# The layer norms' normalisation goes from GpSimd to VectorE, and the chains of work around the scans are placed anew

## The chip, the core and the metric

The kernel runs on one core of one Trainium2 chip. The metric is device microseconds (us) of one launch. Five engines work side by side, each through its own instruction queue in order: TensorE (PE in the profile, PEld for its weight loads), VectorE (DVE), ScalarE (ACT), GpSimd (POOL), and SyncE (SP), which here only issues DMAs. They wait for each other through semaphores, and an instruction that waits holds up everything behind it on its engine.

## The reference

A block of three parts on 4096 tokens (2 batches of 2048) of width 256, all in float32:

```python
x = x + 0.5 * ffn(layernorm(x))      # 8 groups of 512 tokens, each with its own W1, b1, W2, b2; no activation between
x = x + ssm(layernorm(x))
x = x + 0.5 * ffn(layernorm(x))

def layernorm(x):  return (x - mean(x)) / sqrt(var(x) + 1e-5)
def ssm(x):                           # D_INNER = 512 channels, 16 states each
    x_in, z = split(x @ Wi.T + bi)
    u  = silu(conv4(x_in) + conv_b)   # causal, per channel
    dt = softplus(x_in[..., :32] @ Wdt.T + bdt)
    h  = h * exp(dt * A) + dt * Bm * u           # over time, per channel and state
    y  = sum_over_states(h * Cm)
    return (y * silu(z)) @ Wo.T + bo + x * Dv.mean()
```

## The kernel before

**Tiling.** The tokens go in four passes of 1024 (`it` 0 to 3). Each pass has four blocks of 128 channels, so there are 16 blocks `k` (k = 4 it + channel block). A block has 16 scans, s = 0 to 15, each a VectorE instruction over 128 lanes (32 channels by 4 of the 16 states) and 1024 tokens. Block 0 is halved: 32 scans of 512 tokens. That makes 272 scans, numbered i; block k from 1 on holds the scans 16k+16 to 16k+31.

**The ring around a scan.** ScalarE computes the decay `exp` of a scan into one of eight buffers G (L1003, out of RD, a copy of dt that a DMA has spread over the lanes). VectorE scans in that buffer (L1123, with RV, the spread dt*u). TensorE sums the states of four scans into Y (`red`, L1269), and then ScalarE may write the exps of four later scans into those buffers: the exps of scans i+4 to i+7 stand behind `red` of scans i-4 to i-1 in ScalarE's queue and need that sum, so a `red` that comes late on TensorE holds up ScalarE's exps and after them the scans.

**A block's other work**, done while the block before is scanned: projections on TensorE (`xim`, `zm`, `dm`, `um`), their evacuation on ScalarE (`xi`, `z`, `u`, and softplus as `dtr`, `dte`, `dtl`), two small VectorE steps between scans (`dt` L1070, `w` = dt*u L1110), the spreading DMAs (`repd`, `repw` on SyncE's queue), and at s = 3 the product with the gate (`yz` L1132), which needs the last `red` of the block before.

**Layer norms.** There are 24, numbered c = 6 it + 2 ph + hf: pass, place in the block of three (ph 0 to 2), half of 512 tokens. A norm is: on ScalarE the sum (`sum` L812, or from an evacuation) and the squares (`sq` L829, four instructions); then the small steps on [128, 4], `var` (L733), `rstd` (a power with exponent -0.5, L741), `sr` (L746), `off` (L751); then the normalisation `norm` (L758), four instructions of [128, 256] that write XN; then on TensorE the transposes `xt` (L1178), which wait for all four, and ScalarE's copies `xtc` (L849). For the norms 0 to 3, 22 and 23 (`early(c)`), which lie before the scans are in full run or behind them, the steps but `rstd` are on VectorE (`vvar` and so on, `vnorm` L1100). For the 18 norms 4 to 21 all small steps and the normalisation are on GpSimd.

GpSimd also has the second half of the merged FFN weights' mean (`msv` L788, for TensorE's transposes `mt` L1168; the merge `mm` L1158 multiplies W1 by W2 ahead of time), the skip term (`skip` L768 to L776: two small instructions, four of [128, 256] and one of [128, 1024]) and a residual addition (`res` L783).

**What sets the order.** `schedule(do)` is written once and run for each engine, which picks its own stages out of it; so each engine's queue has the stages in the order of this one list. Work besides the scans is written as chains (Python generators). After each scan, `step()` lets every open chain go on to its next `yield`. `PLAN` has the block and the s at which each chain starts, `DTS` and `PROJ` how many scans ahead of its block a block's dt chain and projection chain start, `REST`, `SHIFT` and `WAIT` how many steps a chain rests at certain places, `SENDS` after which scan the DMAs `repw` stand, `RATE` and `STORE` how much work of TensorE and ScalarE a step may let through. Where a stage stands in the list says what it stands behind; when it runs is up to its waits.

Of the kernel before, what the change touches and what calls it, by code (L numbers as in the profile page):

```python
# [6 lines left out]
ALU = mybir.AluOpType  # L7
# [37 lines left out]
        "save": (0, 10)}  # L45
RATE, STORE = 160, 190
FIRST = ["dts", "proj", "outs"]
# [7 lines left out]

PLAN = {"outs": (0, 5), "back0": (0, 12), "back1": (0, 9), "x0": (0, 0), "first0": (0, 0), "front0": (0, 1),
        "x1": (0, 8), "first1": (0, 9), "front1": (0, 11), "ln0": (1, 2), "ln1": (1, 11), "merge0": (2, 6),
        "merge1": (2, 3), "outs3": (3, 3), "skips": (3, 1)}
DTS, PROJ = -20, -25

SENDS, LATE = {6: (0, 1), 13: (2,), 14: (3,)}, {14: (0, 1, 2), 15: (3,)}
REST = 3
SHIFT = 2
WAIT = 7

# [10 lines left out]
def early(c):  # L76

    return c < 4 or c >= 22


def made(stage, c):

    return ("v" if early(c) else "") + stage

# [56 lines left out]
def schedule(do):  # L141
# [76 lines left out]
    def norm(c):  # L218
# [11 lines left out]
        yield 0  # L230
        for part in ("var", "rstd", "sr", "off", "norm"):
            do(part if part == "rstd" else made(part, c), c)
        for _ in range(0 if early(c) else WAIT - 1):
            yield 0
# [227 lines left out]
    a, b, c = norm(0), norm(1), norm(2)  # L462
# [20 lines left out]
    a = half(0, 0)  # L483
# [13 lines left out]
    for i, (k, p, s) in enumerate(UNITS):  # L497
# [8 lines left out]
        if i % 4 == 0:  # L506
            for n in range(i + LEAD, min(i + LEAD + 4, len(UNITS))):
                ko, po, _ = UNITS[n]
# [25 lines left out]
    a, b = back(3, 0), back(3, 1)  # L534
# [15 lines left out]
def build(nc, x, w, wit, wdt, wot, bo, cols, masks, out):  # L550
# [3 lines left out]
    with ctx:  # L554
# [67 lines left out]
        def tokens(c):  # L622
            it, ph, hf = c // 6, c % 6 // 2, c % 2
            return it, ph, hf, X[:, (2 * it + hf) % NX, :, :], LV[:, c % 6, :, :], XN[:, place[c] % 2, :, :]
# [94 lines left out]
        def _(eng):  # L719
            e = Engine(eng, count, sems)  # L720

            def do(stage, *a):
# [24 lines left out]
                elif stage == "off":  # L747
# [4 lines left out]
                                      ).then_inc(sems["off"])  # L752
                elif stage == "norm":
                    c, = a
                    _, _, _, v, lv, xn = tokens(c)
                    e.wait_ge("off", c)
                    for i in range(4):
                        ins = eng.tensor_scalar(xn[:, i, :], v[:, i, :], lv[:, 3, i:i + 1], lv[:, 4, i:i + 1],  # L758
                                                ALU.mult, ALU.add)
                    ins.then_inc(sems["norm"])  # L760
                elif stage == "skip":
# [247 lines left out]
        def _(eng):  # L1009
            e = Engine(eng, count, sems)  # L1010

            def do(stage, *a):
# [82 lines left out]
                elif stage == "vnorm":  # L1095
                    c, = a
                    _, _, _, v, lv, xn = tokens(c)
                    e.wait_ge("voff", c)
                    for i in range(4):
# [248 lines left out]
```

## Time and profile before

| | us |
|---|---|
| median of 3 runs (860.54 to 864.77) | 864.36 |
| the profiled execution's own time | 864.43 |
| its span in the trace, first to last instruction | 862.6 |
| VectorE busy | 666.5 (77%) |
| TensorE busy | 642.4 (74%) |
| ScalarE busy | 598.8 (69%) |
| GpSimd busy | 401.6 (47%) |

The span is split by the scans. The first scan starts at 58.7 us, block 1 at 143.1, block 15 at 785.2, and the last scan ends near 822. In 17 of the 40 slices of the page's second part VectorE is busy nine tenths and more; its idle time there lies in single stretches of 2 to 8 us. Those, and who ended them, are what the views below are asked for. In the rows, `L758` is a line of the kernel before, "xN" the number of instructions in a row that the view has put together, and "[8.30 <-X]" says that the engine was idle for 8.30 us before it and that X ended this.

### The profile page before, as it was taken

To read this page: it belongs to the slowest core of one execution; us is meant where nothing else is said; L and a number is where in the kernel's file an instruction comes from. 1 tells how busy PE (TensorE), PEld (TensorE's weight loads), DVE (VectorE), ACT (ScalarE), POOL (GpSimd) and SP (SyncE) were. 2 spreads that over 40 slices of the span, in tenths; PEclk is the share of its full clock that TensorE was granted. 3 is DMA by queue.
4 is the path that set the end of the run, shared out by engine and by line. 5 is a ranking of instruction groups with operands and counts; after the bars stand their busy time and mean duration, and the time that the engine had idled before them with its cause. 6 is when DMAs were issued, how large, how long until landed. Compare 5 with 4: busy or idle time off the path is not lost.

```text
span 862.6 us, 8004 instructions
## 1 busy us (share of the span) xinstructions
PE 642.4 (74%) x2794; PEld 320.1 (37%) x2794; DVE 666.5 (77%) x412; ACT 598.8 (69%) x1046; POOL 401.6 (47%) x232
## 2 busy tenths in 40 slices
PE   5876677959784759897686859895476797754957
PEld 4643342414241335444242336432221453310635
DVE  2424656699977985999788967989689999699920
ACT  1475577799583957979487848989397689573432
POOL 0003852432596084288997364556881049400000
PEclk9998698879886989999798979998688899785988
DMA  8242345142736150234435240415033324232001
GB/s 308 81 155 65 134 123 219 49 171 75 243 113 229 61 184 1 109 136 149 168 121 197 74 170 1 193 51 196 24 120 124 128 92 152 93 126 93 1 0 49
DMA packets 39432, 103.05 MB, mean 119 GB/s; under 512 B 4000, under 2 KB 12960, under 8 KB 38880
## 3 DMA queue, kind: packets, MB, share of 16 engines
q1 hardware_dynamic: 36832, 94.40, 29.6%
q10 hardware_dynamic: 2560, 8.14, 4.0%
q8 instruction: 22, 0.36, 0.2%
q14 instruction: 18, 0.15, 0.1%
HBM read 23.08 MB, written 4.19 MB: 32 GB/s over the span
## 4 chain that ended last, share of the span: by engine, by line
POOL 27%; ACT 23%; PE 22%; issue 18%; DVE 5%; DMA 3%; ACTq 1%; SPq 0%; POOLq 0%; DVEq 0%
POOL XN L758 12%; ACT G L1003 10%; PE Y L1269 5%; DVE G L1123 4%; POOL LV L741 3%; POOL X L772 3%; PE MB L1195 3%; PE MB L1158 2%; POOL MS L788 2%; PE MB L1236 2%; ACT XN L829 2%; POOL LV L751 2%; ACT XI L923 2%; PE MB L1178 2%; PE MB L1290 2%
## 5 line engine op out<-in xcount | busy, mean ns | idle before, releaser
L1003 ACT ACTIVATE G<-RD,COL 128x1024 f32<-128x1024 f32 (+1 forms) x272 | 276.2, 1087 | 127.8 <-PE Y L1269 124.4
L1123 DVE TENSOR_TENSOR_SCAN G<-G,STT,RV 128x1024 f32<-128x1024 f32 (+1 forms) x144 | 313.7, 2241 | 32.2 <-issue 20.4
L1123 DVE TENSOR_TENSOR_SCAN G<-G,RV 128x1024 f32<-128x1024 f32 (+1 forms) x128 | 272.9, 2192 | 19.3 <-ACT G L1003 16.3
L1269 PE MATMUL Y<-G,RW 128*32 128x512 f32 x1024 | 159.9, 730 | 67.7 <-DVE G L1123 55.1
L758 POOL TENSOR_SCALAR XN<-X,LV 128x256 f32<-128x256 f32 x72 | 137.6, 1922 | 1.9
L733 POOL TENSOR_SCALAR LV<-LV 128x4 f32<-128x4 f32 x18 | 16.7, 929 | 221.9 <-ACT XN L829 221.7
L741 POOL TENSOR_TENSOR LV<-LV,HALF 128x4 f32<-128x4 f32 x24 | 43.4, 1810 | 148.7 <-DVE LV L1078 147.1
L1269 PEld LDWEIGHTS Y<-G,RW 128*32 128x32 f32 x1024 | 31.0, 124 | 163.3 <-issue 90.7
L1236 PE MATMUL MB<-XI,DIAG 128*64 128x512 f32 x248 | 69.8, 691 | 26.9 <-DMA XI<-XI 26.9
L772 POOL TENSOR_SCALAR X<-X,LV 128x256 f32<-128x256 f32 x32 | 82.2, 2578 | 0.8
L1178 PE MATMUL MB<-COL,XN 128*128 128x128 f32 x192 | 33.6, 332 | 61.6 <-POOL XN L758 47.4
L1195 PE MATMUL MB<-MT,XF 128*128 128x256 f32 x256 | 65.9, 393 | 0.6 <-ACT XF L849 0.5
L1214 PE MATMUL MB<-XT,WI 128*128 128x512 f32 x128 | 63.4, 624 | 0.1
L1290 PE MATMUL MB<-WO,ZS 128*128 128x256 f32 x256 | 62.9, 384 | 0.0
L1247 PE MATMUL MB<-XT,WI 128*128 128x512 f32 x128 | 57.8, 599 | 0.0
L1178 PEld LDWEIGHTS MB<-COL,XN 128*128 128x128 f32 x192 | 27.6, 172 | 76.6 <-POOL XN L758 31.4
L1158 PE MATMUL MB<-W 128*128 128x257 f32 x192 | 50.9, 416 | 5.5 <-DMA W<-in_w 4.6
L1195 PEld LDWEIGHTS MB<-MT,XF 128*128 128x128 f32 x256 | 50.1, 197 | 12.3 <-issue 5.1
L829 ACT ACTIVATE XN<-X,LV 128x256 f32<-128x256 f32 x96 | 47.4, 496 | 7.6 <-POOL X L783 4.8
L1290 PEld LDWEIGHTS MB<-WO,ZS 128*128 128x128 f32 x256 | 49.8, 195 | 7.2
L1070 DVE SCALAR_TENSOR_TENSOR DW<-MB,COL,DW 128x512 f32<-128x512 f32 x32 | 22.6, 744 | 38.2 <-ACT DW L981 38.2
L788 POOL TENSOR_SCALAR MS<-MS,MV 128x256 f32<-128x256 f32 x12 | 29.3, 2447 | 39.5 <-DVE MV L1057 39.5
(86 smaller groups left out, 765.7 us busy)
## 6 DMA issues: line engine op xcount, KB each, us to landing
RD<-DW SPq DMA_DIRECT2D x60, 512.0 KB, 3.7
RV<-DW SPq DMA_DIRECT2D x60, 512.0 KB, 3.8
W<-in_w SPq DMA_DIRECT2D x48, 256.5 KB, 4.1
XI<-XI ACTq DMA_DIRECT2D x30, 256.5 KB, 3.8
X<-in_x SPq DMA_DIRECT2D x8, 512.0 KB, 4.3
out<-X SPq DMA_DIRECT2D x8, 512.0 KB, 3.0
G<-in_w SPq DMA_DIRECT2D x2, 1026.0 KB, 9.9
RV<-in_w SPq DMA_DIRECT2D x2, 1026.0 KB, 15.0
```

The lines of the kernel that those rows point to most:

```text
L741: eng.tensor_tensor(lv[:, 3, :], lv[:, 1, :], HALF[:, :], ALU.pow).then_inc(sems["rstd"])
L758: ins = eng.tensor_scalar(xn[:, i, :], v[:, i, :], lv[:, 3, i:i + 1], lv[:, 4, i:i + 1], ALU.mult, ALU.add)
L772: ins = eng.tensor_scalar(v[:, i, :], v[:, i, :], lv[:, 5, i:i + 1], lv[:, 6, i:i + 1], ALU.mult, ALU.subtract)
L829: ins = eng.activation(xn[:, i, :], v[:, i, :], ACT.Square, bias=lv[:, 0, i:i + 1], scale=-256.0, accum_out=lv[:, 1, i:i + 1])
L1003: eng.activation(G[:, i % NG, t0:t1], RD[:, q, t0:t1], ACT.Exp, scale=NAC[:, states(i):states(i) + 1]).then_inc(sems["exp"])
L1123: eng.tensor_tensor_scan(g, g, RV[:, (4 * k + q) % NR, t0:t1], STT[:, idx:idx + 1] if goes_on else 0.0, ALU.mult, ALU.add).then_inc(sems[" ...
L1158: ins = eng.matmul(bank("merge", g, i)[:, 0:257], v[:, 257 + 128 * i:385 + 128 * i], v[:, 0:257], start=(c == 0), stop=(c == 7))
L1178: ins = eng.transpose(bank("xt", c, j)[:, 128 * i:128 * i + 128], xn[:, i, 128 * j:128 * j + 128], ident)
L1195: ins = eng.matmul(o, XF[:, j, 128 * t:128 * t + 128], MT[:, g % NX, j, :], start=(i == 0 and j == 0 and not summed), stop=(i == 1 and j = ...
L1236: ins = eng.matmul(bank("um", k, hf)[64 * g:64 * g + 64, :], DIAG[:, 4 * ct + 2 * g + t, :], XI[:, g, 512 * hf + 2 * t:512 * hf + 2 * t + ...
L1269: ins = eng.matmul(Y[32 * q:32 * q + 32, 512 * h:512 * h + 512], RW[:, states(i + o), :], G[:, (i + o) % NG, 512 * h:512 * h + 512], start ...
L1290: ins = eng.matmul(o, ZS[:, (4 * it + ct) % NZ, 128 * (2 * pr + i):128 * (2 * pr + i) + 128], WO[:, ct, :], start=False, stop=(i == 1 and ...
```

## The change

Two things change. The normalisation of the 18 norms becomes a VectorE stage (`vnorm`) that stands between scans and waits for GpSimd's `off`; GpSimd keeps `var`, `rstd`, `sr` and `off` for these norms. And the numbers that place the chains are others.

```diff
-RATE, STORE = 160, 190
+RATE, STORE = 200, 100
...
-PLAN = {"outs": (0, 5), "back0": (0, 12), "back1": (0, 9), "x0": (0, 0), "first0": (0, 0), "front0": (0, 1),
...
+PLAN = {"outs": (0, 1), "back0": (0, 11), "back1": (0, 13), "x0": (0, 0), "first0": (0, 10), "front0": (0, 1),
...
-DTS, PROJ = -20, -25
+DTS, PROJ = -21, -25
-SENDS, LATE = {6: (0, 1), 13: (2,), 14: (3,)}, {14: (0, 1, 2), 15: (3,)}
-REST = 3
+SENDS, LATE = {9: (0,), 12: (1, 2), 14: (3,)}, {14: (0, 1, 2), 15: (3,)}
+REST = 4
-WAIT = 7
+WAIT = 4
...
-    return ("v" if early(c) else "") + stage
+    return ("v" if early(c) or stage == "norm" else "") + stage
...
-        for part in ("var", "rstd", "sr", "off", "norm"):
+        for part in ("var", "rstd", "sr", "off"):
             do(part if part == "rstd" else made(part, c), c)
-        for _ in range(0 if early(c) else WAIT - 1):
+        for _ in range(0 if early(c) else WAIT):
+            yield 0
+        do("vnorm", c)
+        if not early(c):
             yield 0
...
                 elif stage == "vnorm":
                     c, = a
                     _, _, _, v, lv, xn = tokens(c)
-                    e.wait_ge("voff", c)
+                    e.wait_ge(made("off", c), c)
                     for i in range(4):
                         ins = eng.tensor_scalar(xn[:, i, :], v[:, i, :], lv[:, 3, i:i + 1], lv[:, 4, i:i + 1],
                                                 ALU.mult, ALU.add)
```

In the order's rows an operation's first tile is the one written, `x4` the number in a row; a scan reads there as SCALAR_TENSOR_TENSOR on G and RV. Lines of the changed kernel are 5 lower on these engines (L1118 is the scan, L1095 the normalisation, L1264 `red`, L1173 the transposes).

**VectorE, block 4 into block 5** (`DW` is `dt` or `w`, `ZS` is `yz`). Before:

```order
L1123 SCALAR_TENSOR_TENSOR G<-G,STT,RV 128x1024
L1132 TENSOR_TENSOR ZS<-ZS,Y 128x1024
L1123 SCALAR_TENSOR_TENSOR G<-G,STT,RV 128x1024 x2
L1110 TENSOR_TENSOR DW<-DW 128x1024
L1123 SCALAR_TENSOR_TENSOR G<-G,STT,RV 128x1024 x13
L1070 SCALAR_TENSOR_TENSOR DW<-MB,COL,DW 128x512 x2
```

and changed:

```order
L1118 SCALAR_TENSOR_TENSOR G<-G,STT,RV 128x1024 x3
L1105 TENSOR_TENSOR DW<-DW 128x1024
L1118 SCALAR_TENSOR_TENSOR G<-G,STT,RV 128x1024 x2
L1095 TENSOR_SCALAR XN<-X,LV 128x256 x4
L1118 SCALAR_TENSOR_TENSOR G<-G,STT,RV 128x1024 x8
L1095 TENSOR_SCALAR XN<-X,LV 128x256 x4
L1118 SCALAR_TENSOR_TENSOR G<-G,STT,RV 128x1024
L1095 TENSOR_SCALAR XN<-X,LV 128x256 x4
```

The norms 12, 13 and 4 now stand between scans, and `w` one scan later.

**GpSimd, blocks 2 to 4** (`MS` is `msv`, the rows with DM and BO are a skip term). Before, `msv` of group 5 stands behind both skip terms of the pass:

```order
L788 TENSOR_SCALAR MS<-MS,MV 128x256 x2
L768 TENSOR_SCALAR LV<-LV,DM 128x4
L769 TENSOR_SCALAR LV<-LV,DM 128x4
L772 TENSOR_SCALAR X<-X,LV 128x256 x4
L776 TENSOR_TENSOR X<-X,BO 128x1024
L768 TENSOR_SCALAR LV<-LV,DM 128x4
L769 TENSOR_SCALAR LV<-LV,DM 128x4
L772 TENSOR_SCALAR X<-X,LV 128x256 x4
L776 TENSOR_TENSOR X<-X,BO 128x1024
L788 TENSOR_SCALAR MS<-MS,MV 128x256 x2
```

and changed, behind one:

```order
L783 TENSOR_SCALAR MS<-MS,MV 128x256 x2
L763 TENSOR_SCALAR LV<-LV,DM 128x4
L764 TENSOR_SCALAR LV<-LV,DM 128x4
L767 TENSOR_SCALAR X<-X,LV 128x256 x4
L771 TENSOR_TENSOR X<-X,BO 128x1024
L783 TENSOR_SCALAR MS<-MS,MV 128x256 x2
L763 TENSOR_SCALAR LV<-LV,DM 128x4
```

The same holds for groups 6 and 7 in blocks 6 and 7.

**TensorE, the end of block 6** (XT,WI are projections, COL,XN transposes of a norm, Y is `red`). Before, the transposes of norm 5 stand ahead of the block's last `red`:

```order
L1269 MATMUL Y<-G,RW 32x512 x8
L1204 MATMUL MB<-XT,WI 32x512 x2
L1214 MATMUL MB<-XT,WI 128x512 x2
L1178 MATMUL MB<-COL,XN 128x128 x8
L1204 MATMUL MB<-XT,WI 32x512 x2
L1269 MATMUL Y<-G,RW 32x512 x8
```

and changed, where they have gone to block 5:

```order
L1264 MATMUL Y<-G,RW 32x512 x8
L1199 MATMUL MB<-XT,WI 32x512 x2
L1209 MATMUL MB<-XT,WI 128x512 x2
L1199 MATMUL MB<-XT,WI 32x512 x2
L1264 MATMUL Y<-G,RW 32x512 x8
```

The norms 10 and 11 move like 4 and 5. At the start, the merge of group 2 (8 `mm`) moves from the first half of block 0 to its second half, and the merge of group 3 and the FFN of norm 6 from block 0 to block 1. A block's `dtl` stands one scan earlier and its `dt` where it stood. The stages behind the last scan are the same.

## Rows read from the trace of the kernel before

**Rows 1.** Busy time by stretch (start:end, length, engines, granted clock, DMA).

```profile
0.00:58.00 58.00, 41.11 (x168) 29.06 (x169) 15.93 (x43) 23.61 (x62) 3.43 (x11) 0.97 0.46 166
58.00:143.10 85.10, 63.28 (x238) 32.88 (x238) 44.69 (x49) 58.41 (x138) 42.76 (x35) 0.86 0.42 145
143.10:785.20 642.10, 484.29 (x2152) 223.21 (x2149) 563.81 (x289) 489.87 (x792) 353.35 (x184) 0.87 0.35 125
785.20:862.60 77.40, 53.67 (x240) 34.98 (x240) 42.04 (x33) 26.92 (x56) 2.03 (x2) 0.81 0.04 14
188.40:227.20 38.80, 34.89 (x160) 15.72 (x160) 38.77 (x24) 35.01 (x48) 12.73 (x9) 0.93 0.42 132
```

**Rows 2.** VectorE's waits in 143.1 to 785.2 us: total, times, longest.

```profile
DVE DW L1070 <- ACT DW L981: 23.7, 11, 5.3
DVE G L1123 <- issue: 20.4, 4, 8.3
DVE G L1123 <- ACT G L1003: 14.5, 6, 7.1
DVE ZS L1132 <- PE Y L1269: 13.2, 3, 8.0
DVE DW L1110 <- ACT DW L948: 4.9, 4, 1.3
```

**Rows 3.** Timelines by engine at 300 to 330 us (start, length, instruction, idle before).

```profile
308.30 12.49 POOL L758 TENSOR_SCALAR XN<-X,LV 128x256 f32<-128x256 f32 x4
...
320.94 1.94 PE L1178 MATMUL MB<-COL,XN 128*128 128x128 f32 x8 [9.54 <-POOL XN L758]
...
326.58 4.26 ACT L1003 ACTIVATE G<-RD,COL 128x1024 f32<-128x1024 f32 x4 [11.25 <-PE Y L1269]
...
327.81 2.35 DVE L1123 TENSOR_TENSOR_SCAN G<-G,STT,RV 128x1024 f32<-128x1024 f32 x1 [8.30 <-issue]
```

**Rows 4.** VectorE's other long waits between scans, and TensorE's for GpSimd, 143.1 to 785.2.

```profile
279.39 2.35 DVE L1123 TENSOR_TENSOR_SCAN G<-G,STT,RV 128x1024 f32<-128x1024 f32 x1 [4.69 <-issue]
...
431.40 1.22 DVE L1132 TENSOR_TENSOR ZS<-ZS,Y 128x1024 f32<-128x1024 f32 x1 [4.99 <-PE Y L1269]
...
516.93 2.29 DVE L1123 TENSOR_TENSOR_SCAN G<-G,RV 128x1024 f32<-128x1024 f32 x1 [7.10 <-ACT G L1003]
...
622.40 1.22 DVE L1132 TENSOR_TENSOR ZS<-ZS,Y 128x1024 f32<-128x1024 f32 x1 [8.01 <-PE Y L1269]
...
744.98 4.59 DVE L1123 TENSOR_TENSOR_SCAN G<-G,STT,RV 128x1024 f32<-128x1024 f32 x2 [7.13 <-issue]
...
PE MB L1178 <- POOL XN L758: 47.4, 5, 13.0
```

**Rows 5.** The normalisation on either engine: two groups of the span, two of GpSimd's timeline.

```profile
L758 POOL TENSOR_SCALAR XN<-X,LV 128x256 f32<-128x256 f32 x72 | 137.6, 1922 | 1.9
...
L1100 DVE TENSOR_SCALAR XN<-X,LV 128x256 f32<-128x256 f32 x24 | 8.3, 408 | 0.2
...
129.87 2.19 POOL L758 TENSOR_SCALAR XN<-X,LV 128x256 f32<-128x256 f32 x4
...
598.85 16.28 POOL L758 TENSOR_SCALAR XN<-X,LV 128x256 f32<-128x256 f32 x4
```

**Rows 6.** GpSimd's small steps of norms 12 and 13, and the scans beside the first.

```profile
299.80 1.66 POOL L733 TENSOR_SCALAR LV<-LV 128x4 f32<-128x4 f32 x1 [26.57 <-ACT XN L829]
...
306.04 2.15 POOL L751 TENSOR_SCALAR LV<-LV 128x4 f32<-128x4 f32 x1
...
333.86 0.79 POOL L733 TENSOR_SCALAR LV<-LV 128x4 f32<-128x4 f32 x1 [13.06 <-ACT XN L829]
...
336.11 0.20 POOL L751 TENSOR_SCALAR LV<-LV 128x4 f32<-128x4 f32 x1
...
299.14 20.36 DVE L1123 TENSOR_TENSOR_SCAN G<-G,STT,RV 128x1024 f32<-128x1024 f32 x9
```

**Rows 7.** VectorE's timeline in block 10, around GpSimd's normalisation of 598.85 us.

```profile
587.76 26.63 DVE L1123 TENSOR_TENSOR_SCAN G<-G,RV 128x1024 f32<-128x1024 f32 x12
```

More of the change, by code:

```diff
@@ L54 @@
 AT = {unit: i for i, unit in enumerate(UNITS)}
-PLAN = {"outs": (0, 5), "back0": (0, 12), "back1": (0, 9), "x0": (0, 0), "first0": (0, 0), "front0": (0, 1),
-        "x1": (0, 8), "first1": (0, 9), "front1": (0, 11), "ln0": (1, 2), "ln1": (1, 11), "merge0": (2, 6),
-        "merge1": (2, 3), "outs3": (3, 3), "skips": (3, 1)}
-DTS, PROJ = -20, -25
-SENDS, LATE = {6: (0, 1), 13: (2,), 14: (3,)}, {14: (0, 1, 2), 15: (3,)}
-REST = 3
+PLAN = {"outs": (0, 1), "back0": (0, 11), "back1": (0, 13), "x0": (0, 0), "first0": (0, 10), "front0": (0, 1),
+        "x1": (0, 2), "first1": (0, 1), "front1": (0, 10), "ln0": (1, 1), "ln1": (2, 0), "merge0": (2, 5),
+        "merge1": (1, 6), "outs3": (0, 14), "skips": (3, 10)}
+DTS, PROJ = -21, -25
+SENDS, LATE = {9: (0,), 12: (1, 2), 14: (3,)}, {14: (0, 1, 2), 15: (3,)}
+REST = 4
 SHIFT = 2
-WAIT = 7
+WAIT = 4
 def passes(k):
@@ L752, in do @@
                                       ).then_inc(sems["off"])
[L753 to L760, printed above, removed]
                 elif stage == "skip":
```

## The prediction

> **What bounds the kernel now.** I read the busy times by stretch first, then VectorE's waits, then the timelines of all engines at its longest waits.
>
> By stretch [rows 1], the columns are TensorE, its weight loads, VectorE, ScalarE, GpSimd. From block 1 to block 14 (143.1 to 785.2 us, 642.1 us) VectorE is busy 563.8 us, TensorE 484.3, ScalarE 489.9. Block 2 (188.4 to 227.2) shows the floor: VectorE is busy 38.77 of 38.80 us. So scans in a row are the bound, and what can be won between 143.1 and 785.2 us is VectorE's idle time there, 642.1 - 563.8 = 78.3 us. Ahead of 143.1 us VectorE is idle for most of the first 58 us and for 85.1 - 44.7 = 40.4 us of the next stretch; the tail of 77.4 us is the same code after the change.
>
> Who ends the 78.3 us [rows 2]: the softplus step `dt` waits for ScalarE's logarithm 11 times, 23.7 us; scans wait for "issue" 4 times, 20.4 us, and for their exp 6 times, 14.5 us; `yz` waits for TensorE's sums 13.2 us; `w` waits for silu 4.9 us. That is 76.7 of them.
>
> The views name the last link only. Followed back at one place [rows 3]: GpSimd normalises norm 12 from 308.30 to 320.79 us; TensorE has been idle for 9.54 us when it starts the transposes at 320.94; `red` stands behind them in its queue, so ScalarE's next exps start at 326.58 after 11.25 us without work, and VectorE's scan at 327.81 after 8.30 us idle. The scan does not need norm 12. It waits since TensorE's queue is blocked by a GpSimd step. There are five more such places [rows 4]: VectorE idle for 4.69 us (here TensorE waits for `msv`, which stood behind two skip terms), 4.99, 7.10, 8.01 and 7.13 us. TensorE's waits for the normalisation add to 47.4 us in five waits. The six stalls of VectorE are 8.30 + 4.69 + 4.99 + 7.10 + 8.01 + 7.13 = **40.2 us**, half of the idle time.
>
> **Why GpSimd is late.** The same four instructions take 2.19 us where VectorE is idle and 16.28 us beside scans [rows 5]; the small steps likewise. Norm 12's four run from 299.80 to 306.04 + 2.15 = 308.19, 8.4 us, those of norm 13, in one of VectorE's stalls, from 333.86 to 336.31, 2.4 us [rows 6]. The scans hardly suffer: twelve in a row over 26.63 us, 2.22 us each, with the slowest normalisation of 16.28 us beside them [rows 5, 7].
>
> **Part 1: what the normalisation costs VectorE.** 24 instructions of this kind keep VectorE busy for 8.3 us, 0.346 us each as they overlap, 0.408 us each alone [rows 5]. 18 norms have 72: between 24.9 and 29.4 us. All lie in VectorE's queue between scans, on the path. Norms 6 and 7 lie in block 0, where VectorE has 40.4 us idle [rows 1] (norm 6 stands right ahead of a `w` that waits for ScalarE); I take off 2 x 1.4 and get **+22 us** (20 to 28).
>
> **Part 2: what the new wait costs.** `vnorm` stands four scans behind `off`'s place in the list and waits for GpSimd. Everything behind it on VectorE is scans, and behind these the whole ring. Had it stood there before, norm 12 would have come up two scans into the row of nine, at 299.14 + 2 x 2.26 = 303.7 us [rows 6], and `off` ended at 308.2: 4.5 us late. But a waiting VectorE leaves GpSimd alone, and then the remaining steps run at norm 13's pace: `rstd` was under way and the two behind it take 0.20 us each with small gaps, so about 305, a wait of 1.5 us. In the new order the squares come earlier against the scans, since ScalarE is no longer held up by a blocked TensorE ahead of them, and several norms (14, 15, 17, 20, 21) have five or six scans of room. I count 0.5 us for each of 18, **+9 us**. The ends are 0, and 4.5 us each, 81 us.
>
> **Part 3: the stalls behind the normalisation.** TensorE's transposes now stand behind a step that VectorE has done in its own order, two or three scans before. `msv` of groups 5 and 7 stands behind one skip term, not two, and norms 5 and 11 no longer stand ahead of the last `red` of blocks 6 and 10. Of the 40.2 us I take back 37; the rest is for what is late next. Ends: half, 20, and all.
>
> **Part 4: `dt` and `w`.** 23.7 + 4.9 = 28.6 us in 15 waits, 1.9 us on average [rows 2]. ScalarE's logarithm stands one scan (2.2 us) earlier with `dt` where it was, and `w` one scan later. The two longest waits (to 5.3 us) follow a stall of part 3, which had put ScalarE behind. That would clear nearly all; but the norms' squares of two halves and the output's evacuations now crowd into blocks 4 and 8. I take back **18 us** (0 to 28). What remains of the 78.3 us is then 78.3 - 37 - 18 = 23 us, plus the 9 us of part 2.
>
> **Part 5: the start.** The first half of block 0 loses 8 matmul groups that stood between the transposes of norm 3 and its projections; the second half loses one merge of two and an FFN, which go to block 1. VectorE is idle 40.4 of 85.1 us there. TensorE's load in block 1 grows, but its average share of 484.3 in 642.1 us leaves room. I take **-6 us** (-12 to +4).
>
> **Part 6: scans beside GpSimd.** 137.6 us of GpSimd's work go [rows 5]; at 2.22 us a scan beside it against 38.77 us for block 2 with its 16 scans and other steps, little comes back: **-2 us** (0 to -4). The Trainium skill ("SBUF — State Buffer", where the shared port pair of VectorE and GpSimd is told) has it that the pair is an exclusive lock that a VectorE instruction with two SBUF inputs needs and a GpSimd instruction too, each blocking the other for its whole length. By that rule each of the 72 instructions, 2.19 / 4 = 0.55 us alone, would also hold a scan up, and their removal would return 40 us and not 2. The trace agrees for GpSimd's side (16.28 against 2.19 us) and not for the scans' side.
>
> The DMAs `repw` move: the first now stands behind the four `repd` on SyncE's queue, four to six scans (9 us and more) before the scan that reads it. VectorE's waits for a DMA are not among the rows of any size, so I cost this at nothing; if a transfer of the next block came late, its first scan would show it.
>
> **The sum.** 862.6 + 22 + 9 - 37 - 18 - 6 - 2 = 830.6 us of span. The profiled execution took 864.43 us with 862.6 us of span, 1.8 us more, and is within 0.1 us of the median. Forecast 832.4, rounded **832 us**, 3.7% faster.
>
> **The rivals.**
> - *The new wait takes the place of the old ones* (slower). If ScalarE's squares do not come earlier, `off` is late at most norms, and each lateness is now VectorE's own. For it: norm 12 would have been 4.5 us late as the trace stands. Against it: GpSimd speeds up while VectorE waits, and that caps it. At 3 us each (between 1.5 and 4.5) it is 54 us in place of 9: 832 + 45 = 877 us. It makes the change slower from (32 + 9) / 18 = 2.3 us a norm on.
> - *The stalls move* (no change). TensorE and ScalarE have a part of the idle time in them for their own reasons, for instance in blocks 4, 5, 8 and 9, where output projection, four norms and their FFNs now meet. Then half of 37 + 18 returns as waits for an exp or a sum: 832 + 27 = 859 us. For it: "issue" and exp waits are the least explained. Against it: three quarters load on both, and block 2 ran without a gap.
> - *All clears* (faster still). With VectorE's idle time from block 1 to 14 down to 5 us: 23 + 9 - 5 = 27 us less, 805 us. The same order of time would come of the page's rule above, with 40 us given back by the scans' side: 832 - 38 = 794 us. The trace speaks against the rule; I give the two 0.10 together.
>
> **How the numbers follow.** Forecast 0.72, stalls move 0.10, slower rival 0.08, all clears 0.10. The forecast's own cases go from 812 (all of parts 3 and 4) to 850 (part 3 at 25, part 4 at 8). To leave out no more than 2 in 10, the range runs from 806 to 858. This measurement can tell about 0.5% from no change, 860.0 to 868.7 us. Faster: 0.72 + 0.10 and a part of the second rival, 0.85; the same 0.07; slower 0.08.
>
> **What would show it.** VectorE busy near 666.5 + 25 - 2 = 690 us and its idle time between block 1 and block 14 down from 78 to about 32 us. No wait of TensorE for XN of over 2 us. The `vnorm` group at about 0.35 to 0.41 us an instruction, with an idle time ahead of it, ended by GpSimd's `off`, of some 9 us in all: over 40 us there would be the slower rival. GpSimd busy falls by 137.6 us or more. The blocks 4, 5, 7, 9, 11 and 14 start without stalls of over 3 us. If instead waits for exps stay near 35 us with no GpSimd step behind them, the second rival holds. I would be wrong from the ground up if scans got longer behind the short VectorE steps, for which the trace has no row.

## The result, and the profile after

| | before | changed |
|---|---|---|
| median of the runs (us) | 864.57 | 833.38 (832.38 to 834.11) |
| profiled execution's span (us) | 862.6 | 830.6 |
| VectorE busy | 666.5 (77%) | 700.6 (84%) |
| TensorE busy | 642.4 (74%) | 637.5 (77%) |
| GpSimd busy | 401.6 (47%) | 281.1 (34%) |

The ratio is 0.9633, with a 95% interval from 0.9576 to 0.969: 3.7% faster. The forecast was 832 us, and the span came out at its 830.6. Several terms of the sum were off, though, and cancelled. A few executions are slower at a lower granted clock (one of the changed kernel took 856.0 us at 0.78), and the ratios and the changed kernel's times leave these out.

Busy time by stretch of the changed kernel, cut at the same scans as [rows 1] (columns as there: length, TensorE, its weight loads, VectorE, ScalarE, GpSimd, granted clock):

```profile
0.00:58.00 58.00, 41.54 (x167) 29.27 (x168) 15.92 (x43) 23.45 (x62) 3.42 (x11) 0.94 0.46 165
58.00:143.20 85.20, 55.64 (x188) 21.28 (x187) 47.41 (x55) 57.45 (x126) 26.62 (x25) 0.76 0.35 123
143.20:756.10 612.90, 490.03 (x2200) 234.26 (x2200) 595.33 (x356) 491.38 (x804) 249.06 (x122) 0.89 0.38 134
756.10:830.60 74.50, 50.32 (x240) 33.44 (x240) 41.98 (x33) 26.83 (x56) 2.02 (x2) 0.84 0.04 15
```

Block 1 starts at 143.2 us as before (143.1). The blocks 1 to 14 take 612.9 us in place of 642.1, and the tail 74.5 in place of 77.4. Within the blocks VectorE's idle time fell from 78.3 to 612.9 - 595.3 = 17.6 us, 60.7 us less, and its busy time rose by 31.5 us.

VectorE's waits there, against [rows 2] (total, times, longest; of the 5.0 us for the DMA, 4.6 are block 1's first scan, whose wait ends at 143.19 us and so belongs to the start):

```profile
DVE XN L1095 <- POOL LV L754: 10.1, 9, 2.6
DVE G L1118 <- DMA RV<-DW: 5.0, 2, 4.6
DVE G L1118 <- ACT G L998: 2.3, 3, 1.4
DVE MV L1049 <- ACT MS L852: 2.0, 1, 2.0
DVE DW L1105 <- ACT DW L943: 1.3, 1, 1.3
DVE DW L1065 <- ACT DW L976: 1.2, 1, 1.2
```

`dt`'s 23.7 us are 1.2, `w`'s 4.9 are 1.3, the scans' 34.9 us of waits for "issue" and exps are 2.3, and `yz` does not wait. All six stalls of [rows 3, 4] are gone. The new row at the top is the wait for `off`, 10.1 us in nine times. At norms 13 and 4 it looks like this (timelines of GpSimd and of VectorE; the first three rows and the first of VectorE are norm 13, the others norm 4):

```profile
316.82 2.97 POOL L744 TENSOR_TENSOR LV<-LV,HALF 128x4 f32<-128x4 f32 x1
319.87 1.36 POOL L749 TENSOR_TENSOR LV<-LV 128x4 f32<-128x4 f32 x1
321.32 0.19 POOL L754 TENSOR_SCALAR LV<-LV 128x4 f32<-128x4 f32 x1
...
325.26 1.01 POOL L744 TENSOR_TENSOR LV<-LV,HALF 128x4 f32<-128x4 f32 x1
326.35 0.20 POOL L749 TENSOR_TENSOR LV<-LV 128x4 f32<-128x4 f32 x1
...
321.55 1.38 DVE L1095 TENSOR_SCALAR XN<-X,LV 128x256 f32<-128x256 f32 x4 [0.31 <-POOL LV L754]
...
326.86 1.38 DVE L1095 TENSOR_SCALAR XN<-X,LV 128x256 f32<-128x256 f32 x4 [1.67 <-POOL LV L754]
```

Beside scans `rstd` takes 2.97 us and `sr` 1.36. VectorE's scans end at 321.24 us, and `off`, which starts then, takes 0.19; for norm 4, `rstd` takes 1.01 us and `sr` 0.20 while VectorE waits. So GpSimd's part of such a wait stays short.

In the start two waits are new (VectorE, 58.0 to 143.2 us):

```profile
DVE G L1118 <- DMA RV<-DW: 7.0, 2, 4.6
DVE XN L1095 <- POOL LV L754: 6.8, 1, 6.8
...
122.62 1.38 DVE L1095 TENSOR_SCALAR XN<-X,LV 128x256 f32<-128x256 f32 x4 [6.85 <-POOL LV L754]
...
120.72 0.19 POOL L736 TENSOR_SCALAR LV<-LV 128x4 f32<-128x4 f32 x1 [29.86 <-ACT XN L824]
```

The second is norm 7's. The row names GpSimd's `off`, but that is the last link only: VectorE is idle from 115.77 us, and GpSimd itself waits for ScalarE's squares until 120.7. From there its four steps take 1.9 us. So about 5 us of the 6.85 are a wait for ScalarE. On the other side, the scans of this stretch wait less for their exps than before, 4.3 us in place of this row's:

```profile
DVE G L1123 <- ACT G L1003: 15.3, 4, 6.1
```

And the scans. Their two groups, their durations by form (shortest/median/longest, in ns; first the kernel before, from block 1 on, then the changed one), then VectorE's and GpSimd's timelines:

```profile
L1118 DVE TENSOR_TENSOR_SCAN G<-G,STT,RV 128x1024 f32<-128x1024 f32 (+1 forms) x144 | 319.7, 2277 | 4.8 <-ACT G L998 4.3
L1118 DVE TENSOR_TENSOR_SCAN G<-G,RV 128x1024 f32<-128x1024 f32 (+1 forms) x128 | 276.1, 2215 | 9.3 <-DMA RV<-DW 7.0
...
L1123 DVE TENSOR_TENSOR_SCAN G<-G,RV x112: 2257/2268/4399, 143.1 to 655.9; 128x1024 f32<-128x1024 f32 x112
...
L1118 DVE TENSOR_TENSOR_SCAN G<-G,STT,RV x144: 1249/2321/4392, 100.3 to 790.9; 128x1024 f32<-128x1024 f32 x128, 128x512 f32<-128x512 f32 x16
...
303.20 18.04 DVE L1118 TENSOR_TENSOR_SCAN G<-G,STT,RV 128x1024 f32<-128x1024 f32 x8
...
692.30 26.64 DVE L1118 TENSOR_TENSOR_SCAN G<-G,STT,RV 128x1024 f32<-128x1024 f32 x10
...
80.68 2.34 POOL L771 TENSOR_TENSOR X<-X,BO 128x1024 f32<-128x1024 f32 x1
...
695.06 3.99 POOL L778 TENSOR_TENSOR X<-X,XN 128x1024 f32<-128x1024 f32 x1 [12.67 <-ACT XN L870]
708.69 3.62 POOL L778 TENSOR_TENSOR X<-X,XN 128x1024 f32<-128x1024 f32 x1 [9.65 <-ACT XN L870]
```

All scans together are busy 319.7 + 276.1 = 595.8 us; before, they were busy 313.7 + 272.9 = 586.6. That is 9.2 us more for the same 272 instructions. Eight in a row take 2.26 us each, but ten in a row with two of GpSimd's residual additions beside them take 26.64 - 10 x 2.26 = 4.0 us more: 2 us an addition. The addition is held up too: it takes 3.99 and 3.62 us here, and 2.34 us at 80.68 us, where VectorE is idle.

Two signs of the prediction missed by this. VectorE is busy for 700.6 us and not 690, and GpSimd's busy time fell by 120.5 us and not by 137.6 or more: what it still does took 17 us longer in all, probably since VectorE now pauses less beside it.

### The profile page after: what moved, and what is told of

It is laid out like the page before. It is cut to its first block, busy times and chain, and to the rows that moved or that the text cites. A ratio compares the mean times of both kernels' runs of the same rounds, so it can differ in the third digit from the quotient of the medians.

```text
span 830.6 us, 8007 instructions
## 1 busy us (share of the span) xinstructions
PE 637.5 (77%) x2794; PEld 318.2 (38%) x2794; DVE 700.6 (84%) x484; ACT 599.1 (72%) x1046; POOL 281.1 (34%) x160
## 4 chain that ended last, share of the span: by engine, by line
PE 23%; DVE 19%; ACT 19%; issue 18%; POOL 6%; DMA 3%; ACTq 1%; DVEq 0%; POOLq 0%
DVE G L1118 17%; ACT G L998 8%; PE MB L1190 6%; PE Y L1264 6%; PE MB L1231 3%; DMA XI<-XI 2%; PE MB L1209 2%; PE MB L1188 2%; ACT XN L824 2%; POOL MS L783 2%; ACT XI L918 2%; POOL LV L744 2%; PE MB L1285 1%; ACT XF L844 1%; ACT L900 1%
## 5 line engine op out<-in xcount | busy, mean ns | idle before, releaser
L1118 DVE TENSOR_TENSOR_SCAN G<-G,STT,RV 128x1024 f32<-128x1024 f32 (+1 forms) x144 | 319.7, 2277 | 4.8 <-ACT G L998 4.3
L1118 DVE TENSOR_TENSOR_SCAN G<-G,RV 128x1024 f32<-128x1024 f32 (+1 forms) x128 | 276.1, 2215 | 9.3 <-DMA RV<-DW 7.0
L1264 PE MATMUL Y<-G,RW 128*32 128x512 f32 x1024 | 149.8, 707 | 91.5 <-DVE G L1118 76.9
L1264 PEld LDWEIGHTS Y<-G,RW 128*32 128x32 f32 x1024 | 29.6, 121 | 182.5 <-DVE G L1118 99.2
L1231 PE MATMUL MB<-XI,DIAG 128*64 128x512 f32 x248 | 74.6, 737 | 29.4 <-DMA XI<-XI 29.4
L767 POOL TENSOR_SCALAR X<-X,LV 128x256 f32<-128x256 f32 x32 | 86.6, 2716 | 0.8
L783 POOL TENSOR_SCALAR MS<-MS,MV 128x256 f32<-128x256 f32 x12 | 36.9, 3082 | 91.1 <-DVE MV L1052 91.1
L1190 PEld LDWEIGHTS MB<-MT,XF 128*128 128x128 f32 x256 | 52.7, 207 | 18.3 <-issue 10.1
L1095 DVE TENSOR_SCALAR XN<-X,LV 128x256 f32<-128x256 f32 x96 | 35.5, 433 | 17.3 <-POOL LV L754 16.9
L1231 PEld LDWEIGHTS MB<-XI,DIAG 128*64 128x64 f32 x248 | 19.1, 164 | 74.9 <-issue 74.2
L1153 PE MATMUL MB<-W 128*128 128x257 f32 x192 | 46.3, 390 | 1.6 <-ACT X L878 1.0
L918 ACT ACTIVATE XI<-MB,COL 64x512 f32<-64x512 f32 x64 | 43.3, 677 | 1.4 <-PE MB L1209 0.9
L1153 PEld LDWEIGHTS MB<-W 128*128 128x128 f32 x192 | 35.6, 193 | 15.7 <-issue 7.9
```

The source lines that it names most:

```text
L767: ins = eng.tensor_scalar(v[:, i, :], v[:, i, :], lv[:, 5, i:i + 1], lv[:, 6, i:i + 1], ALU.mult, ALU.subtract)
L918: ins = eng.activation(XI[ps, g, 3 + 512 * hf:515 + 512 * hf], bank("xim", k, hf)[ps, :], ACT.Identity, bias=COL[ps, BI + k % 4:BI + k % 4 ...
L1118: eng.tensor_tensor_scan(g, g, RV[:, (4 * k + q) % NR, t0:t1], STT[:, idx:idx + 1] if goes_on else 0.0, ALU.mult, ALU.add).then_inc(sems[" ...
L1153: ins = eng.matmul(bank("merge", g, i)[:, 0:257], v[:, 257 + 128 * i:385 + 128 * i], v[:, 0:257], start=(c == 0), stop=(c == 7))
L1190: ins = eng.matmul(o, XF[:, j, 128 * t:128 * t + 128], MT[:, g % NX, j, :], start=(i == 0 and j == 0 and not summed), stop=(i == 1 and j = ...
L1231: ins = eng.matmul(bank("um", k, hf)[64 * g:64 * g + 64, :], DIAG[:, 4 * ct + 2 * g + t, :], XI[:, g, 512 * hf + 2 * t:512 * hf + 2 * t + ...
```

## The experiments

Each run stands beside runs of the kernel before on its chip, and the ratio is to those: median 868.5 us for e1_engine to e4_no_adds, 870.6 for e5_res_pe, e6_early_wait and e7_skips_back, 867.0 for e8_adds_pe to e11_w1. The changed kernel itself ran again (a0_after) on the chip of the second group: 834.6 us, ratio 0.959 (0.9538 to 0.9642). Runs on different chips are compared by their ratios.

### The engine alone: e1_engine

```diff
 # the kernel before, all numbers old
-        for part in ("var", "rstd", "sr", "off", "norm"):
+        for part in ("var", "rstd", "sr", "off"):
             do(part if part == "rstd" else made(part, c), c)
-        for _ in range(0 if early(c) else WAIT - 1):
+        for _ in range(0 if early(c) else 4):
+            yield 0
+        do("vnorm", c)
+        for _ in range(0 if early(c) else 2):
             yield 0
```

> The kernel before with one part of the change alone: the 18 normalisations stand on VectorE, four scans behind off, and every number that places chains is the old one, so the transposes stand where they did. Theory (TensorE's queue blocked by the GpSimd step is what costs): the waits of TensorE for XN go from 47 us to a few, four of the six stalls of VectorE (8.3, 5.0, 7.1, 8.0, 7.1 us; not the one behind msv) go, and VectorE pays 25 us for the steps and 1.5 us a norm for the wait: 864 - 35 - 8 of dt + 25 + 20 = about 866 us at worst, 850 at best; I say 856. Rival (the placement is what brought the gain, the engine nothing): 864 + 25 + 20 = 905 us or more.

Measured: 847.58 us, ratio 0.975 (0.9713 to 0.9786). Better than the best I had named. VectorE's wait for `off` in its whole span:

```profile
DVE XN L1095 <- POOL LV L754: 8.6, 9, 1.7
```

8.6 us and not 27: I had put the wait of a norm at three times its size. No wait of TensorE for a GpSimd normalisation is left, with the transposes where they stood. The rival, that the engine brings nothing and the placement all of the gain, is out.

### The numbers alone: e2_numbers

```diff
 # the changed kernel, "norm" on GpSimd again
-        for part in ("var", "rstd", "sr", "off"):
+        for part in ("var", "rstd", "sr", "off", "norm"):
...
-        for _ in range(0 if early(c) else WAIT):
-            yield 0
-        do("vnorm", c)
-        if not early(c):
+        for _ in range(0 if early(c) else WAIT + 1):
             yield 0
```

> The changed kernel with the normalisation back on GpSimd, right behind off, and all the new numbers: the other part alone. Theory: the transposes still wait for a GpSimd step of up to 16 us, so most of TensorE's 47 us of waits for XN stay, but msv behind one skip term (4.7 us), norms 5 and 11 away from the last sum (13 us) and the earlier dt (about 8 us) are won: 864 - 26 = about 840 us. If the numbers fit the new engine alone: 860 us or more. If the numbers were all of it: 833 or less, since VectorE is spared 25 us.

Measured: 892.06 us, ratio 1.0262 (1.0224 to 1.0299), slower than before and far from my 840. TensorE's wait for the normalisation:

```profile
PE MB L1178 <- POOL XN L758: 68.9, 8, 14.8
```

Eight waits in place of five, 68.9 us in place of 47.4 [rows 4]. For 14 of the 18 norms the new numbers put the transposes one to five scans nearer to the squares in the list, which suits a step of 1.4 us on VectorE and not one of up to 16 us on GpSimd. So the two halves of the change do not add: the engine alone brings 2.5%, the numbers alone cost 2.6%, both together bring 3.7 to 4.1%.

### The GpSimd normalisation taken away: e3_no_norm

```diff
 # the kernel before
-                    for i in range(4):
-                        ins = eng.tensor_scalar(xn[:, i, :], v[:, i, :], lv[:, 3, i:i + 1], lv[:, 4, i:i + 1],
-                                                ALU.mult, ALU.add)
-                    ins.then_inc(sems["norm"])
+                    eng.tensor_scalar(xn[:, 0, 0:4], v[:, 0, 0:4], lv[:, 3, 0:1], lv[:, 4, 0:1],
+                                      ALU.mult, ALU.add).then_inc(sems["norm"])
...
-                                            xn[:, i, 128 * j:128 * j + 128],
+                                            xn[:, i, 128 * j:128 * j + 128] if early(c) else ident,
```

> The kernel before with the normalisation of the 18 norms left out (one GpSimd instruction on 4 columns in place of four on 256; the transposes of these norms read a constant). It measures what the GpSimd steps cost in all, with no price on VectorE. Theory: the stalls of 35 us behind them, 10 us of dt's waits behind these, and 2 us of longer scans go: about 815 us, with the 4.7 us behind msv left. Rival (stalls move to other waits of the same queues): half of that, 840 us.

Measured: 837.28 us, ratio 0.963 (0.9579 to 0.968). It lies between theory and rival, nearer the rival. VectorE's waits in its span:

```profile
DVE DW L1068 <- ACT DW L979: 34.9, 11, 11.4
DVE G L1121 <- issue: 10.8, 2, 10.6
```

The stall behind `msv` is there again, and larger (10.6 us in place of 4.69), and `dt` waits as it did. So with the old numbers part of the idle time comes back elsewhere. It also says what the move of the engine costs: e1_engine has 25 us of steps more on VectorE than this kernel and is only 10 us slower. The waits of `dt`, of `w` and of the scans for exps and "issue" add to 82.9 us here and to 61.5 us there, so most of the steps fell into idle time. And leaving the 72 instructions out gave no scan time back: the scans are busy 322.8 + 267.4 = 590.2 us, against 586.6 with them (six scans took over 3 us beside an addition here, three in the kernel before).

### GpSimd's two-input additions cut away: e4_no_adds

```diff
 # the changed kernel
-                    eng.tensor_tensor(v, v, BO[:, :].unsqueeze(1).broadcast_to([P, 4, 256]), ALU.add
-                                      ).then_inc(sems["skip"])
+                    eng.tensor_scalar(v[:, 0, 0:4], v[:, 0, 0:4], 1.0, 0.0, ALU.mult, ALU.add).then_inc(sems["skip"])
...
-                    eng.tensor_tensor(v, v, xn, ALU.add).then_inc(sems["res"])
+                    eng.tensor_tensor(v[:, 0, 0:4], v[:, 0, 0:4], xn[:, 0, 0:4], ALU.add).then_inc(sems["res"])
```

> The changed kernel with GpSimd's two-input additions (bo in the skip term, 8 of 128x1024, and the residual, 6 of 128x1024) cut to four columns each, so these sums are left out. In the trace of the changed kernel scans beside the residual are longer by 1.8 us each and beside the addition of bo by 0.9 us each, 17 us in all, scans beside one-input instructions by 0.15 us. Theory (a two-input GpSimd instruction holds the scan behind it up for its length): scans fall by 17 us, 833 - 15 = 818 us. Rival (the longer scans are chance, or any GpSimd work costs alike): no scan time back beyond 3 us, 830 us.

Measured: 815.54 us, ratio 0.9375 (0.9335 to 0.9415), 2.2 to 2.6% below the changed kernel's. Its scans:

```profile
L1117 DVE TENSOR_TENSOR_SCAN G<-G,STT,RV 128x1024 f32<-128x1024 f32 (+1 forms) x144 | 310.8, 2221 | 5.3 <-ACT G L997 5.0
L1117 DVE TENSOR_TENSOR_SCAN G<-G,RV 128x1024 f32<-128x1024 f32 (+1 forms) x128 | 268.9, 2159 | 8.4 <-DMA RV<-DW 6.6
```

310.8 + 268.9 = 579.7 us, 16.1 us less than 595.8. The 14 additions made the scans longer by that, 1.15 us each; GpSimd's other work was left as it was. The theory holds, and scans are not all that is held up. `w` also reads two tensors; its group in the changed kernel and here:

```profile
L1105 DVE TENSOR_TENSOR DW<-DW 128x1024 f32<-128x1024 f32 (+1 forms) x17 | 23.7, 1392 | 8.1 <-ACT DW L943 8.1
L1104 DVE TENSOR_TENSOR DW<-DW 128x1024 f32<-128x1024 f32 (+1 forms) x17 | 19.5, 1149 | 8.5 <-ACT DW L942 8.5
```

Two of the 17 stood beside an addition of bo and took 3.3 us in place of 1.2, 4.2 us in all. No scan takes over 3 us here; in the changed kernel nine do.

### The residual on TensorE: e5_res_pe

```diff
 # the changed kernel; the way of pass 3 for all passes
-            if it < 3:
-                do("res", it, hf)
...
-                    dst = v if it == 3 else tokens(6 * it + 4 + hf)[5]
+                    dst = v
...
-                    summed = ph == 0 or it == 3
+                    summed = True
```

> The changed kernel with the residual of the second FFN in passes 0 to 2 added by TensorE (one more matmul with the identity for each 128 tokens, as pass 3 does it) in place of GpSimd's addition; the output is the full one. Theory (a two-input GpSimd instruction holds up the scan): the six additions' 9 us of longer scans go, TensorE's 24 matmul groups, 0.4 us each, hide beside scans: 833 - 8 = 825 us. Rival (no hold, or TensorE's added work delays sums): 833 us or more.

Measured: 825.27 us, ratio 0.946 (0.9398 to 0.9522), as the theory had it.

```profile
L1113 DVE TENSOR_TENSOR_SCAN G<-G,STT,RV 128x1024 f32<-128x1024 f32 (+1 forms) x144 | 312.9, 2231 | 3.7 <-ACT G L993 3.7
L1113 DVE TENSOR_TENSOR_SCAN G<-G,RV 128x1024 f32<-128x1024 f32 (+1 forms) x128 | 273.9, 2198 | 8.2 <-DMA RV<-DW 6.8
```

Scans 586.8 us, 9.0 us less, and the time 9 us less.

### The step nearer to off: e6_early_wait

```diff
 # the changed kernel
-        for _ in range(0 if early(c) else WAIT):
+        for _ in range(0 if early(c) else 1):
             yield 0
         do("vnorm", c)
-        if not early(c):
+        for _ in range(0 if early(c) else 4):
             yield 0
```

> The changed kernel with vnorm one scan behind off in the list, not four, and the transposes where they were. Theory (the wait for off is on VectorE's path, and distance hides it): the step comes up three scans, 6.8 us, earlier, so of most of the 18 norms the wait for GpSimd grows by 4 to 7 us less what GpSimd gains by running without scans beside it (up to 6 us): 3 us each, +50 us, 880 us. Rival (VectorE's waits are refunded elsewhere, since TensorE and ScalarE catch up meanwhile): under +15 us.

Measured: 876.34 us, ratio 1.0064 (1.0041 to 1.0087). The wait in its profiled execution, which took 898.1 us, 22 us more than the median, so that the row gives the mechanism more than the size:

```profile
DVE XN L1095 <- POOL LV L754: 84.0, 16, 12.4
```

84.0 us in 16 waits against 16.9 in 10. Three scans of distance are worth 42 us. This is the prediction's slower rival made real: with it, the whole change brings nothing. The waits are not for GpSimd alone: before the longest, 12.4 us, ScalarE's squares are ready only at 171.7 us, and GpSimd's four steps then take 1.9 us. Its speeding up bounds its own part, not the wait for the squares.

### The skip terms back: e7_skips_back, and alone: e10_engine_skips

```diff
-        "merge1": (1, 6), "outs3": (0, 14), "skips": (3, 10)}      # e7: the changed kernel
+        "merge1": (1, 6), "outs3": (0, 14), "skips": (3, 1)}
...
-        "merge1": (2, 3), "outs3": (3, 3), "skips": (3, 1)}        # e10: e1_engine
+        "merge1": (2, 3), "outs3": (3, 3), "skips": (3, 10)}
```

> The changed kernel with the skip terms at their old place in the list (block 3 of a pass, s = 1), so that both stand ahead of msv again. Theory: TensorE's transposes mt wait for msv behind 35 us of skip terms, and the stall of about 5 us returns in block 3 and in block 7: 833 + 8 = 841 us. Rival (the order on GpSimd does not matter with the normalisation gone): 833 us.

> The kernel e1_engine (normalisation on VectorE, old numbers) with one number of the new ones: the skip terms start at s = 10 of a pass's block 3. In e7_skips_back that number was worth 19 us with all the others new. If it carries what the numbers bring (12 us between e1_engine and the changed kernel): 847.6 - 10 = about 837 us. If the other numbers are what counts: 845 us.

Measured: e7_skips_back 854.21 us, ratio 0.9813 (0.9766 to 0.9859), 20 us slower than the changed kernel, more than twice what I had expected. TensorE's and VectorE's waits in it:

```profile
PE MB L1163 <- POOL MS L783: 39.1, 4, 18.3
...
DVE ZS L1127 <- PE Y L1264: 16.9, 4, 8.6
```

Behind both skip terms `msv` holds TensorE for up to 18.3 us, and `yz` waits for the sums (10.8 and 2.0 us in the changed kernel). But e10_engine_skips took 853.34 us, ratio 0.9832 (0.9766 to 0.9899). That is not 10 us faster than e1_engine, and whether it is slower can't be told, as the intervals overlap (0.9713 to 0.9786 there):

```profile
PE MB L1163 <- POOL MS L783: 29.0, 3, 23.3
...
DVE XN L1095 <- POOL LV L754: 14.0, 9, 7.9
DVE ZS L1127 <- PE Y L1264: 13.7, 2, 10.9
```

With the old numbers, the step `mv` of group 7 comes at s = 12 of block 7, behind s = 10 and 11: so both skip terms still stand ahead of its `msv`; and in block 4 the small steps of norm 12 now stand behind them, a wait of 7.9 us. The order on GpSimd's queue counts, one skip term ahead of `msv` and not two, and it takes the other numbers to get it. The number alone has no fixed worth.

### Both additions on TensorE: e8_adds_pe

```diff
 # e5_res_pe, and in the output projection (opa, opm; PART is 1/128)
                     eng.matmul(o, ident, v[:, t, :], start=(i == 0), stop=False)
+                    if half:
+                        eng.matmul(o, PART[:, 0:1].broadcast_to([P, P]), BO[:, :], start=False, stop=False)
...
 # skip on GpSimd
-                    eng.tensor_tensor(v, v, BO[:, :].unsqueeze(1).broadcast_to([P, 4, 256]), ALU.add
-                                      ).then_inc(sems["skip"])
```

> The changed kernel with both of GpSimd's two-input additions done by TensorE, the output complete: the residual as in e5_res_pe, and bo as one more matmul for each 128 tokens of the output projection (a constant 1/128 against bo on all 128 partitions). Theory (each two-input GpSimd instruction holds a scan up): the 17 us of longer scans go nearly whole; TensorE gets 32 matmuls of 0.4 us more, beside scans, and four of them in the tail, +2 us: 835.5 - 17 + 2 = about 819 us. Rival (TensorE's load in blocks 4 and 8 starts to delay sums): 825 us or more, no better than e5_res_pe.

Measured: 819.83 us, ratio 0.9453 (0.9381 to 0.9525). The scans:

```profile
L1111 DVE TENSOR_TENSOR_SCAN G<-G,STT,RV 128x1024 f32<-128x1024 f32 (+1 forms) x144 | 311.0, 2219 | 6.1 <-ACT G L991 4.0
L1111 DVE TENSOR_TENSOR_SCAN G<-G,RV 128x1024 f32<-128x1024 f32 (+1 forms) x128 | 269.2, 2159 | 9.9 <-DMA RV<-DW 7.4
```

580.2 us, 15.6 less than in the changed kernel and 6.6 less than in e5_res_pe, and `w`'s group falls from 23.7 to 19.5 us. Its ratio beats the changed kernel's (0.959, 0.9538 to 0.9642, on another chip), while from e5_res_pe's it can't be told apart, so in time the rival of this run is not excluded.

### The additions cut into quarters: e9_split_adds

```diff
 # the changed kernel
-                    eng.tensor_tensor(v, v, xn, ALU.add).then_inc(sems["res"])
+                    for i in range(4):
+                        ins = eng.tensor_tensor(v[:, i, :], v[:, i, :], xn[:, i, :], ALU.add)
+                    ins.then_inc(sems["res"])      # bo likewise
```

> The changed kernel with the same two additions on GpSimd, each cut into four instructions of 128x256 in place of one of 128x1024 (output complete). It tells what makes them hold up scans. If two inputs do: each quarter holds one scan up for its 0.5 us, the sum stays about 17 us over more scans, 835 us, within 5. If the length of one instruction does, and a short one gets by like the one-input steps at 0.15 us a scan: 17 us become about 6, 825 us.

Measured: 837.79 us, ratio 0.9641 (0.957 to 0.9711), no gain. Scans:

```profile
L1121 DVE TENSOR_TENSOR_SCAN G<-G,STT,RV 128x1024 f32<-128x1024 f32 (+1 forms) x144 | 318.0, 2266 | 4.7 <-ACT G L1001 3.7
L1121 DVE TENSOR_TENSOR_SCAN G<-G,RV 128x1024 f32<-128x1024 f32 (+1 forms) x128 | 278.6, 2234 | 11.3 <-DMA RV<-DW 9.8
```

596.6 us, as with whole additions (595.8). The 56 pieces cost 16.9 us against none (579.7), 0.3 us each, and the longest scan takes 2.8 us in place of 4.4. So the length of one instruction is not what makes the cost. A normalisation instruction of the same 128x256 with one tensor input costs the scans nothing that shows (e3_no_norm), which leaves the two tensor inputs.

### Block 1's w one scan earlier: e11_w1

```diff
 # the changed kernel, in proj(k)
-        for _ in range(REST):
+        for _ in range(REST - (k == 1)):
             yield 0
         yield from after(("dt", k, 0))
         do("w", k, 0)
```

> The changed kernel with the step w of block 1 one scan earlier (after s = 13 of the second half of block 0, as before the change). In the changed kernel block 1's first scan waits 4.6 us for the transfer of dt*u that stands behind w. Theory (the later w is what made it late): the wait falls by one short scan or more, 1.3 to 4.6 us, and the time by as much, 832 us. Rival (w itself waits for ScalarE, so its place does not matter): 835.5 us, unchanged.

Measured: 848.27 us, ratio 0.9766 (0.9704 to 0.9829), 1.3 to 1.8% slower than the changed kernel, 12 to 15 us. VectorE's waits:

```profile
DVE ZS L1127 <- PE Y L1264: 9.5, 2, 7.4
DVE G L1118 <- DMA RV<-DW: 5.4, 5, 2.4
```

The wait of block 1's first scan for the transfer fell from 4.58 us to 1.97, as the theory said. Block 1 started 1.5 us earlier, as `w` itself then waited 4.16 us for ScalarE in place of 1.18: the rival holds in part. But the edit changed more than the place of `w`: a chain that ends one step sooner lets the next go ahead of others, and from there to the first scan of block 2, 54 stages of the list stand one to three scans from where they stood (block 2's silu three scans earlier, the FFN and `mt` later). A sum came late (7.4 us), and exps too. So the run shows a cause of the wait and says nothing of what its removal alone would bring.

## Why the prediction was right

By its own steps (us; the blocks are 143 to 756):

| step | forecast | measured |
|---|---|---|
| part 1, the steps on VectorE | +22 | +23 in the blocks (the group's 35.5 us busy, less the 8.3 of before and 4.1 of norms 6 and 7) |
| part 2, the wait for `off` | +9 | +10.1 in the blocks, 6.8 more in block 0 |
| parts 3 and 4, old idle time | -55 | 78.3 to 17.6 - 10.1 = 7.5: -71 |
| part 5, the start | -6 | 0 |
| part 6, scans beside GpSimd | -2 | +9 |
| tail | 0 | -3 |
| span | -32 | -32 |

That the sum came out to 1 us is luck: parts 3 and 4 gave 16 us more than forecast and the tail 3, and parts 5 and 6 gave 17 less, with 2 more paid in parts 1 and 2. The rows of the table overlap a little; by the busy times, VectorE did 31.5 us more in the blocks where parts 1 and 6 had 20.

The group of part 1, from the changed kernel's page:

```profile
L1095 DVE TENSOR_SCALAR XN<-X,LV 128x256 f32<-128x256 f32 x96 | 35.5, 433 | 17.3 <-POOL LV L754 16.9
```

**What bounds the kernel, and why it stalled: right, and shown.** TensorE's queue blocked by a GpSimd step was the cause: with the engine alone changed (e1_engine) its waits for the normalisation go and 2.5% are won; with the step left out (e3_no_norm) 3.7%.

**Part 1: right.** 23 against 22. In block 0 the steps took 4.1 and not 2.8 us, as norm 6's stood beside an addition of bo (2.73 in place of 1.38 us).

**Part 2: right in the blocks, too small in the start.** With the step one scan behind `off` the change brings nothing (e6_early_wait); four scans bring the wait to 10.1 us in the blocks, at most 2.6 us each. The 9 us were for all 18 norms, though, and norm 7 in block 0 adds 6.85. Four scans of half length are 4.7 us there, and ScalarE's squares were not ready; about 5 us of that wait are theirs. The term had put GpSimd's lateness at a price and ScalarE's at none.

**Parts 3 and 4: mechanism right, size too small.** 71 and not 55 us came back. I kept a third of `dt`'s and `w`'s waits, for fear that blocks 4 and 8 would crowd; 2.5 us are left of 28.6. Here the step that failed is the discount. Two figures behind the range are off as well: with all of parts 3 and 4 the time would be 832 - 3 - 11 = 818 us and not 812, and with 25 and 8 us of them 832 + 12 + 10 = 854 and not 850.

**Part 5: wrong.** The start won nothing. VectorE's idle time in it fell only from 40.4 to 37.8 us, which the steps of norms 6 and 7 took. The scans' waits for exps did fall there, by 11 us, and two new waits took their place. I had costed the later `repw` at nothing, with four to six scans in hand; that holds for full blocks, but block 1's `w` now stands after s = 14 of a half block with scans of 1.2 us, and its first scan waits 4.6 us for the transfer. With norm 7's 6.85 us that is the whole of it. e11_w1 bears out the first of these causes in part (4.58 to 1.97 us) and shows no way to the gain.

**Part 6: wrong, and of the other sign.** I took the scans' pace beside one-input GpSimd steps (2.22 us beside the normalisation, [rows 7]) for all of GpSimd's work. The view of the scans by form shows the exception in the kernel before: its longest scan took 4399 ns, with a median of 2268. That scan stood beside an addition of bo. Before, six of the 14 additions met no scan and three scans took over 3 us; in the changed kernel two met none and nine scans took over 3 us, each beside an addition. The new numbers are not what did it: with the old ones, e1_engine's scans are busy 596.9 us. e4_no_adds and e8_adds_pe measure all the additions at 16 us of scan time and 4 of `w`, e5_res_pe the residual's at 9 us, and e9_split_adds shows that cutting them up does not help.

The trace agrees with the page of the Trainium skill that I had set against it ("SBUF — State Buffer", on the shared port pair as an exclusive lock) for GpSimd's two-input instructions: a scan is up to 2.1 us longer (4392 ns against a median of 2321) beside an addition that alone takes 2.34 us. For one-input ones it does not: 72 of them left out gave no scan time back (590.2 against 586.6 us, e3_no_norm), and the twelve scans of [rows 7] beside one took 2.22 us each, where eight in a row take 2.26. I had rejected the page as a whole from a row on the latter. Its own rival, 40 us back from the 72 removed one-input steps, did not come.

**What the experiments corrected beyond the sum.** I had treated the numbers as small gains of their own, 26 us for them alone in e2_numbers' expectation. They cost 24 us alone and bring 1.2 to 1.6% with the new engine, 10 to 14 us (ratio 0.975 to 0.9633 and 0.959). So the placement suits the new engine's step and not the old one's.

What stays open: which of the new numbers carry those 10 to 14 us, as one number taken by itself reorders the list (e10_engine_skips, e11_w1); and the tail's 3 us, where the stages are the same and TensorE was busy 50.3 in place of 53.7 us at a granted clock of 0.84 in place of 0.81.

## What to carry to other kernels

Follow a wait of the bounding engine back through the queues: a slow step on an engine that is idle half of the time cost 31 us here (what came back when it was left out, e3_no_norm), because something unrelated stood behind its consumer. Moving it onto the bounding engine paid although it added 27 us of work there, once the step stood far enough behind its input that the wait was covered; that distance, and the places of all that follows, have to be chosen for the step's new length. A wait row names only its last link: behind GpSimd's `off` most of norm 7's wait was ScalarE's. And before work of a helper engine is called free, look at the bounding engine's slowest instructions, not at its median.

## What the runs showed of the hardware that I had not expected

- A GpSimd instruction with two tensor inputs (128x1024) makes the VectorE scan beside it up to 2.1 us longer (4392 against 2321 ns), one with one tensor input hardly (72 left out: 590.2 against 586.6 us); 14 such additions cost 16.1 us of scan time (595.8 to 579.7 us), and as much in quarters (596.6 us). A VectorE product of two tensors beside one took 3.3 in place of 1.2 us, and the addition itself up to 4.1 in place of 2.34 us.
- GpSimd's small steps of [128, 4] take longer beside scans (2.97 against 1.01 us for the power, 1.36 against 0.20 for the product), and one that starts when VectorE falls idle takes its short time at once (`off`, 0.19 us).
- A wait of VectorE for GpSimd's four small steps shortens itself by this: with VectorE idle they take 1.9 us (norm 7), beside scans 8.4 us [rows 6]. In the changed kernel no such wait was over 2.6 us in the full blocks. A wait for what comes before these steps is not shortened: 12.4 us in e6_early_wait.
